# The dense layer of batches 0 to 3 moved partly into attention's last two batches, its lo parts all on GpSimd

## What is computed

```python
x = x + attention(x, ...)          # 8 key heads, each shared by 4 query heads, paged cache of 512 keys + 128 new ones
x = x + (x @ W.T + b + coeff[b] * (x @ (2 * mask[b] - 1)))     # the dense layer: W and mask are 512 x 512, mask is int32
x = x + swiglu(x, ...)             # gate, up and down with a rank-16 adapter for each batch
x = x + x @ weight[adapter[b]].T
```

## Time and profile before

| | us |
|---|---|
| median of 3 runs | 1379.77 |
| lowest and highest | 1379.57, 1380.6 |
| the profiled execution | 1377.75 |
| its span, first to last instruction | 1376.0 |

### The profile page before, as it was taken

The page is one execution under the profiler, slowest core; times in us unless marked ns, Lnnn a source line. Parts: engine busy times, 40 slices in busy tenths (PEclk is TensorE's granted clock), DMA queues, the critical chain, the costliest instruction groups (busy, mean ns, idle before and its releaser), DMA issues. The chain is left out here.

```text
span 1376.0 us, 24876 instructions
## 1 busy us (share of the span) xinstructions
PE 1352.7 (98%) x7810; PEld 1192.3 (87%) x7810; DVE 1046.4 (76%) x2132; ACT 841.0 (61%) x2211; POOL 699.5 (51%) x960
## 2 busy tenths in 40 slices
PE   8999999999999999999999999999999889999998
PEld 7898888888988898888998888898888668888886
DVE  7888777877787778777877787778777787758547
ACT  7666666665576566666665666566655575545444
POOL 7766465546555555555555645565545223313204
PEclk9999999999999999999999999999999999999999
DMA  5354235522641364146315720573211164354532
GB/s 197 103 181 154 65 83 176 139 61 76 198 137 30 101 203 107 30 130 202 80 30 152 206 69 15 152 213 91 62 31 43 55 213 139 122 179 158 165 129 84
DMA packets 161994, 163.91 MB, mean 119 GB/s; under 512 B 121488, under 2 KB 129296, under 8 KB 151568
## 3 DMA queue, kind: packets, MB, share of 16 engines
q1 hardware_dynamic: 156144, 128.06, 31.9%
q0 software_dynamic: 5792, 35.13, 7.9%
HBM read 131.71 MB, written 31.46 MB: 119 GB/s over the span
## 5 line engine op out<-in xcount | busy, mean ns | idle before, releaser
L442 POOL TENSOR_SCALAR at_probs<-at_probs,at_row_inv 128x640 f32<-128x640 f32 x256 | 210.0, 821 | 159.8 <-DVE at_row_inv L768 159.8
L530 ACT ACTIVATE at_pT_hi<-at_ps 128x512 fp32r<-128x512 f32 x320 | 186.7, 605 | 105.3 <-PE at_ps L65 52.3
L762 DVE CUSTOM_DVE_ANT_0 at_scores<-at_ps,at_mask,at_inv_rms 128x640 f32<-128x640 f32 x256 | 220.1, 878 | 32.7 <-PE at_ps L65 32.3
L575 ACT ACTIVATE at_probs<-at_scores,at_neg_max 128x640 f32<-128x640 f32 x256 | 211.8, 835 | 50.4 <-DVE at_neg_max L762 50.2
L710 DVE TENSOR_TENSOR at_pT_lo<-at_ps,at_pT_hi 128x512 fp32r<-128x512 f32 x320 | 212.3, 685 | 28.6 <-ACT at_pT_hi L530 28.6
L570 ACT ACTIVATE at_square<-at_ps 128x128 bf16<-128x128 f32 x256 | 67.2, 277 | 172.8 <-DVE at_w_q L741 152.5
L957 PE MATMUL at_ps<-ident,at_probs 128*128 128x128 f32 x1280 | 160.6, 273 | 1.8 <-POOL at_probs L442 1.8
L63 PE MATMUL at_ps<-at_kT_hi,at_qT_hi 128*128 128x320 f32 x512 | 158.4, 309 | 1.5 <-DVE at_neg_max L762 0.8
L65 PE MATMUL at_ps<-at_kT_hi,at_qT_lo 128*128 128x320 f32 x512 | 158.2, 309 | 0.0
L64 PE MATMUL at_ps<-at_kT_lo,at_qT_hi 128*128 128x320 f32 x512 | 158.1, 309 | 0.0
L957 PEld LDWEIGHTS at_ps<-ident,at_probs 128*128 128x128 f32 x1280 | 145.3, 141 | 10.4 <-POOL at_probs L442 2.7
(11 more groups left out here) (216 smaller groups left out, 3646.1 us busy)
## 6 DMA issues: line engine op xcount, KB each, us to landing
kT_pages<-shared SPq DMA_DIRECT2D x14, 1024.0 KB
v_pages<-shared SPq DMA_DIRECT2D x14, 1024.0 KB
at_k_raw<-kT_pages SPq DMA_DIRECT2D x56, 256.0 KB, 3.6
at_v_raw<-v_pages SPq DMA_DIRECT2D x56, 256.0 KB, 4.3
sw_wgu_raw<-in_sw_gu SPq DMA_DIRECT2D x22, 512.0 KB, 3.5
staging<-in_L_cond_Wq SPq DMA_DIRECT2D x8, 1024.0 KB
staging<-in_L_cond_Wo SPq DMA_DIRECT2D x8, 1024.0 KB, 4.8
shared<-in_mask_Bx4096x_ik SPq DMA_DIRECT2D x7, 1024.0 KB, 5.6
```

What stands on the lines that cost most here:

```text
L442: pool.tensor_scalar(probs[:, h, :], probs[:, h, :], row_inv[:, h:h + 1], 1.0, ALU.mult, ALU.mult).then_inc(probs_done, 1)
L530: act.activation(out, src, ACT.Copy).then_inc(done, 1)
L575: act.activation(probs[:, h, :], scores[h % 2][:], ACT.Exp, bias=neg_max[:, h:h + 1], scale=-1.0, accum_out=row_sum[:, h:h + 1]).then_inc( ...
L762: dve.tensor_tensor_reduce(out=scores[h % 2][:], in0=slot(h), in1=mask[:, b, :], scale=inv_rms[b % 2][:, h:h + 1], scalar=3.0e38, op0=ALU. ...
```

## The change

Buffers that only one layer used become common, so that the dense layer can begin in the attention block: one PSUM tensor for both blocks; x1's parts take attention's xT buffers; the dense parts take the buffers of attention's weights (`hi[0]`, `lo[0]`, `hi[1]`) and of its query parts (`lo[1]`, so GpSimd waits for the last score before lo parts of batch 1); mask 3 takes the tile of `k_raw` and `v_raw`, which later holds the down weights `wd_raw` of the three chunks in flight; the bias and the A-ranks take `u_q` and `w_q`. In the last attention group the engines' queues then get:

- batch 4: weights(0,0), (0,1) as before; batch 5: VectorE weights(0,2), (0,3) earlier in the batch; ScalarE hi parts (0,0), (0,1); GpSimd the four lo parts of batch 0 behind its normalise calls.
- batch 6: PE transposes x1(0), x1(1); ScalarE hi(0,2), hi(0,3), row sum 0, hi of x1(0), x1(1); VectorE weights(1,0), (1,1) and the lo parts of x1; GpSimd all lo parts of batches 1 and 2.
- batch 7: PE product(0) before the transposes, x1(2) before `times_v`, product(1) and x1(3) before `output`, product(2) behind it; ScalarE hi(1,0..3) and hi(2,0) before its part of `probs_T`; VectorE weights(1,2), (1,3), (2,0) before its part, and (2,1) to (3,1) later.

In the second block remain product(3), hi(3,2), hi(3,3), weights(3,2), (3,3), the lo parts of batch 3 and on, and row sum 3. ScalarE's and PE's order around `tokens` and `ranks` is changed. The down weights of chunk 0 may be loaded only when all lo parts of batch 3 are made. All lo parts of the dense layer are GpSimd's, lo(4,1) and lo(4,3) too. The order below is that of the file: SP, GpSimd, ScalarE, VectorE, PE of attention, the class, then SP, GpSimd, ScalarE, VectorE, PE of the second block.

```diff
+        xT_hi, xT_lo = dense.x_hi, dense.x_lo
...
+        wqT_hi, wqT_lo = dense.hi[0], dense.lo[0]
+        wkvT_hi, wkvT_lo = (dense.hi[1][:, 2 * n:2 * n + 2, :].rearrange("p a (c d) -> p (a c) d", d=2 * D) for n in range(2))
...
+        k_raw, v_raw = ([dense.masks[3][:, (2 * n + j) * L:(2 * n + j + 1) * L].rearrange("p (c d) -> p c d", d=D) for j in range(2)] for n in range(2))
...
+        qT_hi, qT_lo = ([dense.lo[1][:, 2 * n + j, :] for j in range(2)] for n in range(2))
+        u_q, w_q = (t[:].rearrange("p (h d) -> p h d", h=G) for t in (dense.bias_sb, dense.a_raw))
...
             dense.load_mask(sp, 2)
+            sp.wait_ge(q_rot_done, HK * B)
+            dense.load_bias(sp)
+            loads.a_ranks(sp, 0)
+            sp.wait_ge(kc_done, HK * B)
+            sp.wait_ge(v_cache_done, HK * B)
+            dense.load_mask(sp, 3)
...
                     if last and b == 3:
                         prepare_dense()
+                    if last and b == B - 3:
+                        for c in range(DC):
+                            dense.part_lo(pool, 0, c)
+                    if last and b == B - 2:
+                        pool.wait_ge(scores_in_psum, HK * B * G)
+                        for at in range(1, 3):
+                            for c in range(DC):
+                                dense.part_lo(pool, at, c)
...
+                    if last and b == B - 1:
+                        for c in range(DC):
+                            dense.part_hi(act, 1, c)
+                        dense.part_hi(act, 2, 0)
                     probs_T(g, b, 0)
...
                         probs_T(g, b, c)
+                    if last and b == B - 2:
+                        dense.part_hi(act, 0, 2)
+                        dense.part_hi(act, 0, 3)
+                        dense.row_sums(act, 0, square[:, 0:G, :].rearrange("p h d -> p (h d)"))
+                    if last and b == B - 1:
+                        dense.x1_hi(act, 2, X1_BANK[2])
+                        dense.part_hi(act, 2, 1)
+                        for at in range(1, 3):
+                            dense.row_sums(act, at, scores[at % 2][:, 0:DM])
...
                     hi(oT_hi[:], bank(o_bank(b)), pv_done, upto(g, b, KC, KC), oT_hi_done)
                     if more:
                         exps(g1, b1, 2)
+                    if last and b == B - 2:
+                        dense.x1_hi(act, 0, X1_BANK[0])
+                    if more:
                         exps(g1, b1, 3)
+                    if last and b == B - 2:
+                        dense.x1_hi(act, 1, X1_BANK[1])
+                    if last and b == B - 1:
+                        dense.part_hi(act, 2, 2)
+                        dense.x1_hi(act, 3, X1_BANK[3])
+                        dense.part_hi(act, 2, 3)
+                        for c in range(2):
+                            dense.part_hi(act, 3, c)
...
                         cached_keys(g2, b2)
+                    if last and b == B - 3:
+                        act.wait_ge(q_in_psum, HK * B)
+                        dense.part_hi(act, 0, 0)
+                        dense.part_hi(act, 0, 1)
...
+                    if last and b == B - 1:
+                        dense.weights(dve, 1, 2)
+                        dense.weights(dve, 1, 3)
+                        dense.weights(dve, 2, 0)
                     probs_T(g, b, 0)
                     probs_T(g, b, 1)
...
                         probs_T(g, b, c)
                     if last and b == B - 1:
-                        dense.weights(dve, 1, 2)
+                        dense.x1_lo(dve, 2, X1_BANK[2])
+                        dense.weights(dve, 2, 1)
...
+                    if last and b == B - 3:
+                        dense.weights(dve, 0, 2)
                     if more2:
                         turn_q(g2, b2, 0)
                         turn_q(g2, b2, 1)
...
                         inverse(g1, b1, 0)
+                    if last and b >= B - 3:
+                        for at, c in {B - 3: ((0, 3),), B - 2: ((1, 0),)}.get(b, ()):
+                            dense.weights(dve, at, c)
...
                         mask_and_max(g1, b1, 2)
                         inverse(g1, b1, 1)
                     attended(g, b)
+                    if last and b == B - 1:
+                        dense.weights(dve, 2, 2)
+                        dense.weights(dve, 2, 3)
+                        dense.add(dve, 0)
+                        dense.x1_lo(dve, 3, X1_BANK[3])
+                        dense.weights(dve, 3, 0)
+                        dense.add(dve, 1)
+                        dense.weights(dve, 3, 1)
                     if more:
                         mask_and_max(g1, b1, 3)
                         inverse(g1, b1, 2)
+                    if last and b == B - 2:
+                        dense.x1_lo(dve, 0, X1_BANK[0])
+                    if more:
                         inverse(g1, b1, 3)
+                    if last and b == B - 2:
+                        dense.weights(dve, 1, 1)
+                        dense.x1_lo(dve, 1, X1_BANK[1])
...
-                    if last:
-                        for at, c in {B - 4: ((0, 0), (0, 1)), B - 3: ((0, 2), (0, 3)), B - 2: ((1, 0), (1, 1)),
-                                      B - 1: ((1, 3), (2, 0), (2, 1), (2, 2))}.get(b, ()):
-                            dense.weights(dve, at, c)
-                    add_y(g, b)
+                    if last and b == B - 4:
+                        dense.weights(dve, 0, 0)
+                        dense.weights(dve, 0, 1)
+                    add_y(g, b, last)
...
+                    if last and b == B - 1:
+                        dense.product(pe, 0)
                     probs_T(g, b, 0)
...
                     for c in range(2, KC):
                         probs_T(g, b, c)
+                    if last and b == B - 1:
+                        pe.wait_ge(dense.x1_done, 2)
+                        dense.x1_turn(pe, 2, X1_BANK[2])
                     times_v(g, b, 0)
...
                         project_kv(*following(g2, b2))
+                    if last and b == B - 2:
+                        dense.x1_turn(pe, 0, X1_BANK[0])
+                        pe.wait_ge(kn_done, HK * B)
+                        dense.x1_turn(pe, 1, X1_BANK[1])
+                    if last and b == B - 1:
+                        dense.product(pe, 1)
+                        dense.x1_turn(pe, 3, X1_BANK[3])
                     output(g, b)
+                    if last and b == B - 1:
+                        dense.product(pe, 2)
...
+X1_BANK = [4, 5, 5, 2] + [7] * QUAD
+DENSE_BANK = [4, 0, 1, 0] + [7] * QUAD
...
+        self.masks.append(ctx.enter_context(nc.sbuf_tensor("kv_raw", [P, DC * DM], F32)))
...
+    def part_hi(self, act, b, c):
+        act.wait_ge(self.done, b * DC + c + 1)
+        if b >= 2:
+            act.wait_ge(self.in_psum, b - 1)
+        act.activation(self.hi[b % 2][:, c, :], self.rows(b)[:, c, :], ACT.Copy).then_inc(self.hi_done, 1)
+    def part_lo(self, pool, b, c):
+        pool.wait_ge(self.hi_done, b * DC + c + 1)
+        pool.tensor_tensor(self.lo[b % 2][:, c, :], self.rows(b)[:, c, :], self.hi[b % 2][:, c, :].bitcast(F32),
+                           ALU.subtract).then_inc(self.lo_done, 1)
+    def x1_turn(self, pe, b, n):
+        pe.wait_ge(self.x1_ready, b + 1)
+        for c in range(DC):
+            ins = pe.transpose(self.bank(n)[:, c * S:(c + 1) * S], self.xres[:, b, c * P:(c + 1) * P], self.ident[:])
+        ins.then_inc(self.x1_in_psum, 1)
+    def x1_hi(self, act, b, n):
+        act.wait_ge(self.x1_in_psum, b + 1)
+        act.activation(self.x_hi[:, :, b * S:(b + 1) * S], self.turned(n), ACT.Copy).then_inc(self.x1_hi_done, 1)
+    def x1_lo(self, dve, b, n):
+        at = slice(b * S, (b + 1) * S)
+        dve.wait_ge(self.x1_hi_done, b + 1)
+        dve.tensor_tensor(self.x_lo[:, :, at], self.turned(n), self.x_hi[:, :, at].bitcast(F32), ALU.subtract).then_inc(self.x1_done, 1)
+    def row_sums(self, act, b, junk):
+        act.wait_ge(self.x1_ready, b + 1)
+        act.activation(junk, self.xres[:, b, :], ACT.Identity, scale=self.minus_coeff[:, b:b + 1],
+                       accum_out=self.sign_bias[:, b:b + 1]).then_inc(self.sums_done, 1)
+    def product(self, pe, b):
+        at = slice(b * S, (b + 1) * S)
+        pe.wait_ge(self.x1_done, b + 1)
+        if b >= 2:
+            pe.wait_ge(self.x2_done, b - 1)
+        for c in range(DC):
+            pe.wait_ge(self.lo_done, b * DC + c + 1)
+            ins = three_pass(pe, self.bank(DENSE_BANK[b]), self.x_hi[:, c, at], self.x_lo[:, c, at], self.hi[b % 2][:, c, :], self.lo[b % 2][:, c, :],
+                             c == 0, c == DC - 1)
+        ins.then_inc(self.in_psum, 1)
+    def add(self, dve, b):
+        dve.wait_ge(self.bias_loaded, 16)
+        dve.wait_ge(self.sums_done, b + 1)
+        dve.wait_ge(self.in_psum, b + 1)
```

(59 more changed lines are left out.)

240 lines of the change are left out of this document (69 added, 171 removed).

## The result

The changed kernel takes **1386.19 us** (median of 5, 1384.13 to 1387.47) against 1379.57 us for the kernel before, run beside it (median of 5, 1377.59 to 1380.6). The ratio is 1.0050, with a 95% interval of 1.0036 to 1.0065: 6.6 us slower. Forecast were 1377.1 us and a range that ended at 1380.8. Both the sign and the range were wrong.

A forecast was written before the change was run, and what follows sets the result against it. TensorE's lost time bounded the stretch from attention's last-but-one batch to the first gate product: 15.5 us, forecast 11.25. With gate 1's new wait, -4.2 + 1.5 = -2.7 us, so 1377.1 us, range 1374.0 to 1380.8.

The forecast's parts named there:

- Part 1: Before batch 7: moved work mostly fits existing waits; 0.8 us lost instead of 2.8, product(0) starts near 1084.0.
- Part 2: Batch 7 to the block's end: a new 2.1 us wait before times_v(7,0); 3.7 us lost in all.
- The barrier takes 0.3 as now: At attention's block end, behind product(2) near 1105.1: the barrier costs 0.3 us, unchanged.
- Part 3: After the barrier: waits at product(3) 2.5 us and ranks(1) 2.75; 6.75 us lost, gate 0 starting 4.2 earlier overall.
- Part 4: At gate 1: SP issues chunk 1's weights late, giving a new wait of 1.4 + 0.1 us.
- the 3.24 MB in a row: SP's loads from mask 4 through chunk 1: 8.5 us at 380 GB/s plus 2.8 fixed, landed near 1125.7.
- rival B: At gate 1: late SP loads at 187 GB/s, a 7.3 us wait, slower at 1383.0 us; chance 0.11.
- Part 5: Before product(4): lo(4,1) and lo(4,3) pass from VectorE to GpSimd, changing the time by 0.
- rival A: Whole change as worked out, -4.4 to -1.0 us with bounds, so 1375.4 to 1378.8 us; chance 0.49.

The follow-up runs named there:

- e_best2: e_best with tokens(3) put ahead of gate_up_weights(0) on ScalarE and VectorE; 1373.95 us, ratio to the kernel before 0.9958.
- e_dvelo: The changed kernel with VectorE, not GpSimd, making the four lo parts of batch 3; 1384.74 us, ratio to the kernel before 1.0035.
- e_drain: The changed kernel with the last two lo parts of batch 2 made by VectorE, not GpSimd; 1384.54 us, ratio to the kernel before 1.0044.
- e_sp: The changed kernel with SP loading weights 1 and B-ranks 1 ahead of mask 4, down ranks and mask 5; 1381.78 us, ratio to before 1.0022.
- e_warm: The changed kernel with identity transposes keeping TensorE at work in its three longest waits; 1384.11 us, ratio to the kernel before 1.0039.
- e_pad: The changed kernel with only its buffers moved, by padding and placement of gate and up weights; 1382.65 us, ratio to the kernel before 1.0023.
- e_best: e_all plus the edits of e_dvelo and e_pad; 1374.81 us, ratio to the kernel before 0.9963.
- e_all: The changed kernel with the edits of e_drain and e_sp, and ScalarE's zero rows at the block's head; 1378.83 us, ratio to before 1.0002.
- b_shift: The kernel before with only 832 bytes of padding ahead of SwiGLU's gate and up weights' hi parts; 1380.72 us, ratio to before 1.0014.

## Why the prediction was wrong

**Part 1 was right.** product(0) ran unwaited from 1086.5, where 1084.0 + 2.5 was forecast, and the x1 transposes filled their wait.

**Part 2 was right but for one term.** The three weights parts beside the lo parts took 4.62 us, 1.54 each for my 1.6, and TensorE waited 1.81 us for my 2.1. The five lo parts of GpSimd took 7.58 us, 1.52 each. The rule of the Trainium skill (SBUF — State Buffer, SBUF: two separate sides), an exclusive lock for the whole instruction, would give 1.27 + 0.66 = 1.93 for a pair; this trace has 1.5, so the measurement decides against it as a sum. That an instruction of VectorE can stand behind one of GpSimd is in line with it: the ad_cols part in e_best2 took 1.32 us for 0.22. And e_dvelo shows that the pair gains nothing over VectorE alone. product(2) closed TensorE's part at 1107.3, where 1105.1 + 2.5 was forecast.

The step that failed is the sentence **"The barrier takes 0.3 as now"**. The block's end took 2.2 us more, because GpSimd's drain ends 3.7 us after its last instruction, and the change gives GpSimd work up to the block's end. I had costed the barrier from a row in which another engine came last. e_drain shows it.

**Part 3 was right in mechanism, and a term was missing.** The chain lo(3,3), down weights 0, gate weights 0, zero rows, tokens(3) came as described, with a wait of 3.1 us for 2.75, and the load itself took 2.7 us for 3.3. But ranks(1) then ran at half clock (1.1 us more). Gate 0 started 53.3 us after the start of batch 6 (1072.33), not 50.7: 1.6 us sooner than before instead of 4.2.

**Part 4 was the right wait at half its size.** Gate 1 was forecast at 1127.9 + 2.5 and came at 1135.4, 5 us later. Three terms make the 5. First, 2.0 us are inherited: SP issued mask 4 at 1118.87, where 1114.4 + 2.5 was forecast, because the block began late. Second, **the 3.24 MB in a row were costed at 380 GB/s.** From that issue to the landing of chunk 1 it took 12.9 us for 11.3, and the mean over these 12.9 us is 308 GB/s:

```profile
1118.87:1131.75 12.88, 9.75 (x48) 8.40 (x47) 4.54 (x8) 4.80 (x11) 0.00 (x0) 0.87 0.95 308
```

That makes 3.96 MB, so up to 0.7 MB of what SP had issued before and behind the row moved in the same time. Third, **the consequence was read one step short**: behind gate_up_weights(1) on ScalarE stands silu(0), with a table load of 1.28 us, and gate 1 needs its bank. From the landing to gate 1 it took 3.7 us for 2.2. Then came 1.6 us at half clock. This is **rival B** in place and in sign, but not in size or mechanism: B wanted under some 290 GB/s and a wait of 7.3 us, and the wait was 3.1. Its chance was 0.11, because I set the full microseconds of the earlier trace rows against it; a full microsecond is not the mean over twelve.

**Part 5** (nothing) held in the changed kernel, where the 0.58 us before product(4) went. That was luck: gate 1 was so late that VectorE had time. In e_sp and e_best2, where it is sooner, the wait is back at 1.05 and 1.88 us.

Together the forecast missed 5.95 us between batch 5 and the end of this stretch (+3.25 for -2.7). The rows give them: 5.0 at gate 1, with the block's end in it, and 1.6 at half clock, less the 0.6 before product(4). The bounds that the prediction names for parts 2 and 3 would add up to -5.3 and -0.7, not to rival A's -4.4 and -1.0; neither reaches what was measured.

**What no part and no rival had.** Two causes. The granted clock was 1.00 in every row that I read, with waits of up to 1.7 us in the stretch, and I let waits grow to three microseconds without asking whether that would last; e_warm puts some 2 us on it. And "the buffers are shared" was read as a question of dependences only. That every buffer behind them moves was costed at nothing, without a bound. It costs 3.5 us by the medians (e_pad), over half of the 6.6, and by the traces 1.9 in attention and some 2 in SwiGLU. With that undone the change still loses 3.9 us against before. With the loads' order, the drain, the zero rows and the lo parts mended as well, its idea is worth 4 to 5 us, more than I gave it.

## What to carry to other kernels

Give every wait that a change adds or lengthens its second price: what stands behind it in the waiting engine's queue, and what a fall of TensorE's clock behind it would cost (up to 1.6 us each time here). Read the drains at a block's end before moving work to an engine that was idle there. When a change moves buffers, compare the spacing of untouched matmuls in the two traces first. A pace that differs where nothing was reordered may be a matter of placement, and a pad of a few hundred bytes tells. Where the intervals of two medians overlap, read the gain as the distance between two matmuls that both traces have.

## What the runs showed of the hardware

- **GpSimd's drain** ended 3.6 to 3.7 us after its last instruction (before, changed, e_drain), VectorE's, ScalarE's and TensorE's within 0.1 us of it.
- **The granted clock** fell from 1.00 to 0.50 (from 2.4 to 1.2 GHz) for some 3 us around the ends of TensorE's waits of 2.5, 3.1 and 3.1 us in the changed kernel. It did so at 11 of the 13 waits of 2.4 us and more in the five kernels that have such waits, and not at 2.94 us in e_sp and at 3.03 us before gate 1 in e_pad. The batch 7 wait of 1.8 us is the same in all nine kernels of the changed kind, and the clock fell behind it in two (e_sp, e_best). In e_all it fell behind another of 1.8 us; behind waits of 1.5 us in e_best and e_best2 it did not. So the wait's length alone does not decide. With transposes in the three long waits it stayed at 1.00.
- **The place of buffers** in SBUF changed the spacing of gate and up products from 0.2287 to 0.2337 us, 2.2%: a pad of 832 bytes and nothing else brought the slower pace (b_shift). The Trainium skill (SBUF — State Buffer, SBUF: two separate sides) says that TensorE never waits on another engine at its ports. These runs neither show nor refute that. It may be TensorE's own operands that meet, but the query projection changed its pace though its own had not moved. They show only that the place of a buffer has a price.
- **GpSimd beside VectorE**, both reading SBUF alone, took 1.5 us for a lo part and a weights part (changed kernel, batch 7); VectorE alone took 1.35 us for both (0.65 and 0.70 in e_dvelo).
